# A mixture-of-experts layer sorted per pair of batches, and one batch's gather moved into the next block

## The reference, cut to what matters

```python
h = _layernorm(x, axis=-1) * (1 + cb) + sb
# _L0_ffn_ref: 8 experts, 128 -> 512 -> 128, two experts for each row
router_probs = jax.nn.softmax(router_logits, axis=-1)
expert_weights, expert_idx = jax.lax.top_k(router_probs, 2)
expert_weights = expert_weights / (expert_weights.sum(axis=-1, keepdims=True) + 1e-09)
h = jax.nn.gelu(einsum('bnc,efc->bnef', x, expert_w1) + expert_b1, approximate=False)
out_all = einsum('bnef,ecf->bnec', h, expert_w2) + expert_b2
out = (out_k * expert_weights[..., None]).sum(axis=2)      # the two chosen experts only
x = x + gb * out
```

## Time and profile before

| | |
|---|---|
| median of 3 runs | 1514.68 us |
| lowest, highest | 1509.36, 1516.99 us |
| the profiled execution | 1507.7 us, span 1506.0 us |
| mean granted TensorE clock | 0.910 |
| TensorE matmul, weight load | 1243.9 us (83%), 778.0 us (52%) |
| DVE, ACT, POOL | 981.3 us (65%), 914.2 us (61%), 529.1 us (35%) |
| expert loop | first tile through at 207.1 us, last at 409.9 us |
| projecting block | from 414.0 us to about 500 us |

### The profile page before, as it was taken

How to read it: one execution, slowest core, us unless ns; L and a number is a source line. 1 busy time by engine, 2 the same in 40 slices (tenths; PEclk the granted TensorE clock), 3 DMA queues, 4 the chain that set the end, 5 groups by cost and what they waited for, 6 DMA issues and landing times. The chain is left out here.

```text
span 1506.0 us, 26566 instructions
## 1 busy us (share of the span) xinstructions
PE 1243.9 (83%) x8185; PEld 778.0 (52%) x8186; DVE 981.3 (65%) x2622; ACT 914.2 (61%) x1319; POOL 529.1 (35%) x588
## 2 busy tenths in 40 slices
PE   6996768988896589999999999989998996665560
PEld 4875668978853123333433343333344874465560
DVE  5563466666678398888888788878887574420222
ACT  4562623423365588988888888878886664233330
POOL 6245745466286411221112111211120024444444
PEclk9998879999988799999999999999999897787885
DMA  9800022322246432222222122222200501112222
GB/s 265 231 1 28 26 63 85 101 77 75 77 153 185 115 48 36 35 35 36 37 37 36 39 36 40 41 40 40 40 8 8 169 15 48 51 32 67 77 60 74
DMA packets 114787, 100.44 MB, mean 67 GB/s; under 512 B 10882, under 2 KB 99424, under 8 KB 114656
## 3 DMA queue, kind: packets, MB, share of 16 engines
q1 hardware_dynamic: 101256, 78.64, 22.0%
q0 software_dynamic: 8192, 16.79, 4.0%
q10 hardware_dynamic: 5208, 3.43, 0.9%
HBM read 54.51 MB, written 44.30 MB: 66 GB/s over the span
## 5 line engine op out<-in xcount | busy, mean ns | idle before, releaser
L2413 ACT ACTIVATE probs<-scores_ps 128x1024 f32<-128x1024 f32 x512 | 507.4, 1027 | 81.8 <-PE scores_ps L2440 77.2
L2440 PE MATMUL scores_ps<-q_pack,k_pack 64*128 64x512 f32 x1024 | 245.4, 492 | 43.0 <-ACT probs L2413 21.2
L2457 PE MATMUL pv_ps<-probs,v_pad 128*32 128x512 f32 x2048 | 274.7, 609 | 0.1
L2440 PEld LDWEIGHTS scores_ps<-q_pack,k_pack 64*128 64x128 f32 x1024 | 96.2, 184 | 315.6 <-issue 170.1
L2340 POOL TENSOR_TENSOR squares<-sparse_scores 128x512 f32<-128x512 f32 x32 | 41.0, 1280 | 472.9 <-DVE sparse_scores L2578 472.9
L1391 ACT ACTIVATE hidden_experts<-pre_experts 128x512 f32<-128x512 f32 x94 | 59.3, 631 | 130.5 <-DVE pre_experts L1325 67.6
L2650 DVE TENSOR_SCALAR_CACHE_REDUCE junk<-sparse_scores,at 128x1024 f32<-128x1024 f32 x96 | 122.8, 1279 | 3.4
L1413 PE MATMUL up_ps_experts<-x_t_experts,up_weights_now_experts 128*128 128x128 f32 x752 | 108.2, 290 | 16.8 <-DVE up_weights_now_experts L1320 6.6
L1413 PEld LDWEIGHTS up_ps_experts<-x_t_experts,up_weights_now_experts 128*128 128x128 f32 x752 | 95.8, 200 | 22.6 <-DVE up_weights_now_experts L1320 16.5
L3210 POOL DMA_INDIRECT expert_rows_dram<-expert_input_tail,send_to_tail x64 | 61.5, 961 | 127.0 <-DVE send_to_tail L3352 108.7
L1420 PE MATMUL down_ps_experts<-weights_t,hidden_experts 128*128 x736 | 99.9, 280 | 0.0
(11 more groups left out here) (406 smaller groups left out, 2414.9 us busy)
## 6 DMA issues: line engine op xcount, KB each, us to landing
q_pack<-q_pieces_dram SPq DMA_DIRECT2D x120, 64.0 KB
k_pack<-k_pieces_dram SPq DMA_DIRECT2D x120, 64.0 KB
expert_rows_dram<-zeros SPq DMA_DIRECT2D x1, 6400.0 KB, 23.2
x_rows_experts<-expert_rows_dram SPq DMA_DIRECT2D x25, 256.0 KB
expert_rows_dram<-y_rows_experts SPq DMA_DIRECT2D x46, 128.0 KB
q_pieces_dram<-q_pieces_prep SPq DMA_DIRECT2D x8, 512.0 KB, 3.6
k_pieces_dram<-k_pieces_prep SPq DMA_DIRECT2D x8, 512.0 KB, 5.7
expert_rows_dram<-zeros SPq DMA_DIRECT2D x1, 2560.0 KB, 18.2
```

What stands on the lines that cost most here:

```text
L2413: act.activation(probs[:, kt % 2, 2 * pair : 2 * pair + 2, c * 512 : c * 512 + 512], scores_ps[n % 2][:].rearrange("p (h t) -> p h t", h=2 ...
L2440: ins = pe.matmul(scores_ps[n % 2][:, head * 512 : head * 512 + 512], k_pack[group % 2][rows, pair, kt * P : kt * P + P].bitcast(F32R), q_ ...
L2457: ins = pe.matmul(pv_ps[32 * j : 32 * j + 32, c, :], v_pad[:, group % 2, kt, j, :], probs[:, kt % 2, j, c * 512 : c * 512 + 512], start=(k ...
```

## The change

Layer 0's rows are sorted for a pair of batches at once: 2 x 2 x 1024 row copies take at most 32 + 7 tiles, rounded up to 40 (a multiple of `UNROLL`), 80 in all; the loop has 20 steps. The count of an expert covers both batches, so `positions` adds the first batch's counts to the second's rows (8 more matmuls), and the small operations of `index` and `experts_of_tiles` have other shapes. The cleared part of `expert_rows` has 88 tiles instead of 100.

In the expert loop the tiles of a pair are released when both of its batches have been sent. POOL gathers batch 0 after the first pair's 40 tiles are stored, one gather a tile; it sums it; it gathers batch 1 with no pacing; it sums that; both inverse roots come last. Batch 2's gather is gone from there: in the projecting block it stands ahead of `pick.0`, with its sum and statistics (`comb.2 stats.2`) moved from near the head of the order to just ahead of `rstd.2`. DVE's statistics of batch 0 are taken at step 16, those of batch 1 after the loop.

```diff
-BATCH_TILES = (2 * T // P + E - 1, E * CAPACITY // P)
+UNROLL = 4
+PAIRS_OF_BATCHES = B // 2
+ROW_TILES = (-(-(2 * 2 * T // P + E - 1) // UNROLL) * UNROLL, E * CAPACITY // P)
+ROW_PARTS = (PAIRS_OF_BATCHES, B)
 TRASH_AT, TRASH_STEP = 6, 8
-UNROLL = 4
 
 
 class ExpertRows:
 
 
     def __init__(self, nc, layer):
-        self.tiles = BATCH_TILES[layer]
-
-        self.trash = B * self.tiles * P
+        self.tiles = ROW_TILES[layer]
+
+        self.trash = ROW_PARTS[layer] * self.tiles * P
         self.cleared = self.trash + (2 * UNROLL * P if layer == 0 else 0)
...
-                    for c in range(2):
-                        for m in range(NT):
-                            pe.matmul(to[:, c * E : c * E + E], g.ones_b[:], sel[:, c * NT + m, :], start=(m == 0), stop=(m == NT - 1))
+                    for m in range(2 * NT):
+                        pe.matmul(to[:, 0:E], g.ones_b[:], sel[:, m, :], start=(m == 0), stop=(m == 2 * NT - 1))
                     for c in range(2):
                         at = 2 * E + c * NT * E
                         pe.matmul(to[:, at : at + NT * E], g.before[:], sel[:, c * NT : c * NT + NT, :].rearrange("p n e -> p (n e)"), start=True, stop=False)
+                        for m in range(c * NT):
+                            pe.matmul(
+                                to[:, at : at + NT * E].rearrange("p (n e) -> p n e", e=E), g.ones_b[:], bc(sel[:, m, :], NT), start=False, stop=False
+                            )
                         for m in range(NT - 1):
...
-    STEPS = B * moe.tiles // UNROLL
-    AHEAD = -(-moe.tiles // UNROLL)
+    STEPS = PAIRS_OF_BATCHES * moe.tiles // UNROLL
+    AHEAD = moe.tiles // UNROLL
     HALF = UNROLL // 2
 
-    STATS_AT = (13, 20)
+    STATS_AT = 16
...
-                    pool.sem_inc(rows_here, moe.tiles)
-                pool.sem_inc(rows_here, max(moe.tiles, 2 * UNROLL))
-                for b in range(B - 1):
-                    pool.wait_ge(y_free, b * (2 * AHEAD) + (2 * AHEAD + 1))
-                    tile_at[0] = max(tile_at[0], (b + 1) * moe.tiles)
-                    gather(pool, g, picked, b, [(k, n) for k in range(2) for n in range(NT)], g.rows_picked, apart=next_tile)
-                    if 1 <= b <= EARLY:
-                        pool.wait_ge(var_ready, b)
-                        g.ln1.invert(pool, b - 1).then_inc(rstd_ready, 1)
+                    if b % 2 == 1:
+                        pool.sem_inc(rows_here, moe.tiles)
+                pool.sem_inc(rows_here, 2 * UNROLL)
+                pool.wait_ge(y_free, 2 * AHEAD + 1)
+                tile_at[0] = max(tile_at[0], moe.tiles)
+                for b in range(EARLY):
+                    gather(pool, g, picked, b, [(k, n) for k in range(2) for n in range(NT)], g.rows_picked, apart=next_tile if b == 0 else None)
                     pool.wait_ge(g.rows_picked, (b + 1) * (16 * 2 * NT))
-                    if b < EARLY:
-                        for part in weighted_sum(g, picked, b, NT):
-                            part(pool, step)
-                        pool.sem_inc(summed, 1)
+                    for part in weighted_sum(g, picked, b, NT):
+                        part(pool, step)
+                    pool.sem_inc(summed, 1)
+                for b in range(EARLY):
+                    pool.wait_ge(var_ready, b + 1)
+                    g.ln1.invert(pool, b).then_inc(rstd_ready, 1)
                 pool.wait_ge(rstd_ready, EARLY)
...
+                with dve.Fori(0, STATS_AT) as i:
+                    tiles_of(i, [])
+                parts = stats(0)
+                done = STATS_AT
+                for at in range(0, len(parts), UNROLL):
+                    tiles_of(done, parts[at : at + UNROLL])
+                    done += 1
                 with dve.Fori(done, STEPS) as i:
                     tiles_of(i, [])
+                for part in stats(1):
+                    part()
...
-pick.0 cols center.0 center.1 norm.0 comb.2 pick.1 norm.1 turn.0 pick.2 colk turn.1 stats.2 ht.0 vrow pick.3 ht.1 q.0 rowk sqk.1 p0.0.0 pick.4
-square.0.0 sv.1 skk.1 rest.0.0 pick.5 skc.1 k.0 sqd.1 k.1 p0.0.1 p2.0.0 sqout.1 rstd.2 square.0.1 svk.1 qkout.0.0 q.1 p0.1.1 heads rest.0.1 square.1.1
+pick.0 cols center.0 center.1 norm.0 pick.1 norm.1 turn.0 pick.2 colk turn.1 ht.0 vrow pick.3 ht.1 q.0 rowk sqk.1 p0.0.0 pick.4
+square.0.0 sv.1 skk.1 rest.0.0 pick.5 skc.1 k.0 sqd.1 k.1 p0.0.1 p2.0.0 sqout.1 comb.2 stats.2 rstd.2 square.0.1 svk.1 qkout.0.0 q.1 p0.1.1 heads rest.0.1 square.1.1
...
                     all_parts = [(k, n) for k in range(2) for n in range(NT)]
+                    if i == 0:
+                        gather(pool, g, picked, EARLY, all_parts, g.rows_picked)
                     n = len(all_parts) // PICKS
                     gather(pool, g, picked, B - 1, all_parts[i * n : i * n + n], last_picked)
...
                 def combine(b):
+                    if b == EARLY:
+                        dve.wait_ge(g.rows_picked, (EARLY + 1) * (16 * 2 * NT))
                     if b == B - 1:
```

66 lines of the change are left out of this document (28 added, 38 removed).

## The result

The changed kernel took 1519.3 us (median of 10 runs, 1516.88 to 1523.0) against 1515.53 of the kernel before in 10 runs beside it: a ratio of **1.0032, 95% interval 1.0018 to 1.0047**, some 5 us slower. The forecast was 1512.8, some 2 us faster. The profiled execution of the changed kernel took 1521.3 us (span 1519.5), 13.6 above that of before; since the medians differ by 3.8, I compare stretches, and take a stretch for changed only where the change touches it.

What follows compares the result with a forecast made beforehand. TensorE was taken to bound the expert loop, POOL's queue the projecting block; -23.4 - 14.7 + 13 + 2.8 + 20 + 0.4 = -1.9 us on the 1514.68 median gave 1512.8, range 1500 to 1523.

Steps and rivals of the forecast that it cites:

- the front's 0.4: Front: eight more bf16 matmuls for the positions, about +0.4 us.
- Items 1 to 3: Expert loop: 12 fewer tiles -23.4 us, old gather bursts gone -14.7, new burst +13, sums on POOL 0.
- item 2: Gather bursts in the loop: two old ones vanish, -14.7 us; batch 1's 16 unpaced gathers cost +13, between 5.5 and 20.
- rival (c): Loop stands still during the burst of 16 gathers: 20 us in place of 13, total 1520, chance 0.10.
- a sign of being wrong: Burst costing under 6 or over 18 us, or a projecting block growing by under 10 us.
- Item 4: Loop's tail: batch 1's statistics and inverse root behind the last tile, +2.8 us, between 0 and 5.2.
- Item 5: Projecting block: batch 2's 16 gathers delay everything behind them on POOL's queue, +20 us, from 16 to 23.
- Item 6: Projecting block: batch 2's sum on DVE, moved later, makes work behind it 13 us later; cost 0, hidden by POOL's lateness.
- Rival (d): Projecting block: the moved DVE sum adds to the gathers' delay, +11 us, total 1526, chance 0.12.
- The wait ahead of batch 3's sum: Projecting block: DVE's wait for batch 3's gathers ends 59 us into the block.
- Rivals (a) and (b): Projecting block hides the gathers, +20 near 0, 1493, chance 0.08; a burst costs once, 5.5 for 13, 1505, chance 0.12.
- The rule that spoke against the change: DVE copies stall GpSimd's DMA issue, 620 ns becoming some 3100: the loop's 16 gathers cost 50 us, change loses 28.

Runs made afterwards that it cites:

- stats18: Changed kernel with batch 0's statistics at steps 18 and 19 instead of 16 and 17; ratio 1.0037.
- statsend: Changed kernel with both batches' statistics behind the loop, which is then one repeated body without unrolled steps; ratio 1.0048.
- invhead: Changed kernel with batch 1's inverse root moved from POOL's end of the loop to its head in the projecting block; ratio 0.9997.
- nogather2: Changed kernel with batch 2's 16 gathers, and DVE's wait for them, left out of the projecting block; 1360.26 us, ratio 0.9925.
- nogather2_old: Changed kernel without batch 2's 16 gathers, with batch 2's sum and statistics back at the head of the projecting block; block 93.37 us.
- order: Changed kernel with batch 3's last four gathers ahead of batch 2's inverse root, batch 3's sum and statistics ahead of POOL's first source tile; ratio 1.0095.
- after_again: Changed kernel itself, unedited, as control on a chip of the second kind; ratio 1.0011 to the kernel before.
- beforemove: Kernel before (92 tiles, sorted per batch) with only batch 2's gather and sum moved to the projecting block; 1389.25 us, ratio 1.0124.

## Why the prediction was wrong

By its items; the stretches sum to +5.0 with the front's 0.4, where it had -1.9.

- **Items 1 to 3, the loop**: -25.1 forecast, -21.4 measured. The pace held: tiles 24 to 40 take 30.85 us, 1.93 each. With 23.4 for the tiles and 14.7 for the old bursts, 16.7 are left for the new one (17.6 by its own rows) where **the +13 of item 2** stood: mis-sized by 3.7. The bound of 20 held it, and rival (c) was nearer: only tiles 62 and 63 were finished within it, 339.72 and 348.15, not half the pace. By tiles 60 to 68 it is 20.8, above the 18 that the prediction had named as a sign of being wrong. The step that failed is the scaling: seven and nine gathers cost 0.8 and 1.0 us each, sixteen 1.1, so the cost grows a little faster than the number, and I had scaled back towards the smaller one for the statistics in the nine. stats18 and statsend show that the statistics had no part in it. The reading behind that choice was wrong too: the wait of 3.57 us in the earlier trace rows is not at the entry of the unrolled steps (tile 52, 316.40) but at tile 55, and it ended 0.13 us after TensorE's report of a product shown as ended 5.2 us earlier (322.29, raised at 327.46).
- **Item 4, the tail**: +2.8 forecast, **+6.8 measured**, above its own upper bound of 5.2. Its 4.0 us and the 3.7 of the burst would each have turned the sign alone; here it is the reasoning that failed, and not only a size. The bound counted the work (statistics and inverse root, of which 1.7 us showed behind the other engines) and left out what POOL's queue does behind its last work: a drain of 5.27 us. Before it lay hidden beside the last tiles; it had to be looked for in the rows of the queues, since the busy rows do not show it. invhead, which moves one instruction of 1.7 us, gets all of it back.
- **Item 5, the block's gathers**: +20 forecast, +19.2 measured, 19.1 by experiment. Right, and for the reason given. The spacing in the block was 1.30; POOL's last root moved by 17.8, and the rest is the 1.4 us by which what lies behind it was longer (45.9 for 44.5).
- **Item 6, the moved sum**: 0 forecast, 0 measured beside the gathers (they end 36.7 us in, the statistics of batch 2 at 34). The step behind it was incomplete: DVE's lateness also holds POOL's inverse root, which made nogather2's block 9.8 us longer than nogather2_old's, and only the gathers it came with hide that. Rival (d) is out as a price: its sign, the DVE work from the `sparse_v` addition to batch 3's sum, went from 14.4 us before to 22.6, short of its 26, and order shows that this sum's start does not carry the block.
- **The wait ahead of batch 3's sum**: forecast to end 59 us in. The sum started 57.4 us in, without a wait. DVE came to it straight from its own queue, 10 us later than the 47 forecast:

```profile
437.78 1.23 DVE L1910 TENSOR_TENSOR sparse_v<-ps_prep,bias_rows 128x1024 f32<-128x1024 f32 x1 [1.26 <-issue]
...
459.20 1.28 DVE L1938 TENSOR_SCALAR shift_rows_prep<-ps_prep,k_max_prep 48x1024 f32<-48x1024 f32 x1 [3.20 <-PE ps_prep L2141]
460.41 1.82 DVE L1695 TENSOR_TENSOR v<-v,gates 128x1024 f32<-128x1024 f32 x1
```

The last gather was issued at 454.86; with the 4.6 us that the last one took before (448.55 to 453.19), it landed, as an estimate, 56.5 us in, just ahead of DVE. The time was nearly right, by luck: another engine set it.
- **Rivals (a) and (b)** are out: the block hid nothing, and the burst did not cost 5.5 on this kind of chip. On the second kind (b) is nearer than the forecast: 1.5 us.
- **The rule that spoke against the change** (the Trainium skill, SBUF — State Buffer, "SBUF: two separate sides"): in after_again, where DVE kept its pace, the 16 gathers take 0.94 to 1.03 us each beside ten DVE copies of 0.41 to 0.47 us, none some 3 us. The Trainium skill has such a DMA blocked there until the copy ends, so with copies this short the 3.1 us of the estimate was the wrong figure to take from it. The stall did not show, there or in the changed kernel's burst (0.94 to 1.06); what was hurt was the other engines, not the DMA's issue.

All in: -21.4 + 6.8 + 19.2 = +4.6. The saving in tiles is there on either kind of chip (on the second, beforemove's loop takes 185.0 us and after_again's 160.0), and POOL's queue in the block and at the loop's end takes it back.

## What to carry to other kernels

Moving gathers from one stretch to another moves their time in POOL's queue and does not remove it: ask in which stretch POOL has slack, and pace them by the consumer's steps there. Before a piece of work is put behind a loop, look at the drains at the end of the block; the engine that works last pays its drain in the open. And a version in which one edit is undone can hit a second wait that the edit had hidden (nogather2), so undo them in pairs. A wait that the profile gives no releaser for is not yet a wait for nothing: look up when the semaphore was raised.

## What the runs showed of the hardware

- Gathers issued by POOL without a pause (1.25 us apart, 16 of them) held back the other engines in all five traces on chips of the first kind: 17.6 us by tiles 61 to 64 in the changed kernel, 18.9 to 20.8 by tiles 60 to 68, with 24 to 35 us of waits without a releaser on ACT and DVE. On two chips of the second kind they cost 1.5 us. At 1.47 us apart the cost halved.
- In that burst the semaphores that TensorE raises for its products came 1 to 18 us after the ends shown, and the last three or four within 0.34 us. DVE and ACT waited for these. Beside shorter rows of POOL's DMAs they were late by less (up to 4 us beside five in a row); in the traces of the second kind that were looked at, after_again and nogather2, by 0.01 to 0.02 us throughout. Why they are late stays open.
- The chips differ by 9% for the same kernel (1508 against 1370 us). Of the 149 us between the changed kernel's two traces, 109 lie behind the attention (344.1 and 235.0 us) and some 21 each in the front (210.7 and 190.1) and the loop (181.4 and 160.0); the projecting block (113.4 and 112.5) and the attention (659 and 662) are nearly the same. The mean granted clock behind the attention is 0.75 and 0.90.
- POOL's drain at a block's end took 5.27 us behind sums and an inverse root, 6.58 in the kernel before; TensorE's took 1.97, ACT's 0.52, DVE's 0.21 to 0.33, SP's 0.01.
- A DVE copy of 128x512 took 0.41 us beside a gather (337.45) and 1.73 us beside POOL's addition of 128x1024 (335.00, the addition from 334.03 to 336.44).
